# Cross-attention and expert layer: all halves routed four tasks to a slot, six scattered two to a step, and a small buffer cleared behind each scatter of the last two

## What is computed

```python
def reference(x, ctx_768, mask, ...):
    # attention: queries from the normed x; keys and values from the context and from the normed x
    x = x + xattn(ctx_768, layernorm(x), mask, ...)      # 4 heads of 64, key norm, softmax over 77 + 1024 keys
    # experts: each token goes to 8 of 64
    h = layernorm(x).reshape(4096, 256)
    scores = sigmoid(h @ gate_w.T)
    sfc = scores + gate_bias
    group_scores = top_k(sfc by 8 groups of 8, 2).sum()  # the best 4 groups are kept
    topk_idx = top_k(sfc in those groups, 8)
    weights = scores[topk_idx] / sum * 2.5
    pos = running count of the tokens of each expert     # over 256: left out
    buf[e, pos] = h[token]                               # 64 x 256 rows
    y = (silu(buf @ w_gate) * (buf @ w_up)) @ w_down
    return x + add up of y * weight by token
```

## Time and profile before

| what | us |
|---|---|
| median of three runs | 1085.38 (1082.44 to 1087.95) |
| span of the profiled execution | 1168.4 |
| busy in it: TensorE | 906.8 (78%) |
| VectorE | 655.7 (56%) |
| GpSimd | 581.3 (50%), of it the 256 scatters 251.2 |
| ScalarE | 463.0 (40%) |

### The profile page before, as it was taken

The page is one execution under the profiler, slowest core; times in us unless marked ns, Lnnn a source line. Parts: engine busy times, 40 slices in busy tenths (PEclk is TensorE's granted clock), DMA queues, the critical chain, the costliest instruction groups (busy, mean ns, idle before and its releaser), DMA issues.

```text
span 1168.4 us, 13234 instructions
## 1 busy us (share of the span) xinstructions
PE 906.8 (78%) x3848; PEld 626.7 (54%) x3848; DVE 655.7 (56%) x1956; ACT 463.0 (40%) x930; POOL 581.3 (50%) x522
## 2 busy tenths in 40 slices
PE   3869999999999999999964973957308999889300
PEld 2545666556656656656532542846207888777200
DVE  4475647875789775888652743743533443333206
ACT  3734675545755646664430521333103333222000
POOL 3530231204755635655665073155554888888850
PEclk9879999999999999999986995968658999999755
DMA  7739602012221422101261102000428999999689
GB/s 249 267 111 386 218 3 72 20 31 90 77 78 58 132 84 87 55 23 67 78 239 54 37 29 87 24 24 9 171 88 244 308 312 188 158 159 152 70 231 392
DMA packets 85335, 150.77 MB, mean 129 GB/s; under 512 B 14090, under 2 KB 53050, under 8 KB 83216
## 3 DMA queue, kind: packets, MB, share of 16 engines
q1 hardware_dynamic: 54543, 112.32, 27.8%
q0 software_dynamic: 30720, 37.61, 16.3%
HBM read 69.19 MB, written 97.45 MB: 143 GB/s over the span
## 4 chain that ended last, share of the span: by engine, by line
PE 48%; DVE 13%; issue 11%; POOL 8%; another core or an unknown queue 7%; DMA 7%; ACT 4%; POOLq 0%; SPq 0%; ACTq 0%; DVEq 0%
PE ps_o L1257 15%; PE ps_u L1154 6%; POOL sum L1111 4%; PE ps_s L1233 4%; PE ps_s L1235 4%; PE ps_u L1177 4%; DMA out_rows<-again,row_ids 3%; PE ps_u L1269 2%; PE ps_o L1252 2%; POOL out_rows L1111 2%; PE ps_u L1321 2%; DVE mp L1580 2%; PE ps_u L1165 2%; DMA sum<-again,row_ids 2%
## 5 line engine op out<-in xcount | busy, mean ns | idle before, releaser
L1044 POOL DMA_INDIRECT slot_rows<-rows,slot_idx x256 | 251.2, 981 | 312.0 <-issue 137.5
L1580 DVE TENSOR_REDUCE mp<-ps_u 128x1 f32<-128x512 f32 x256 | 165.1, 686 | 103.2 <-remote 49.6
L1450 ACT ACTIVATE probs<-ps_s 128x512 f32<-128x512 f32 x256 | 139.9, 596 | 176.6 <-PE ps_s L1235 105.4
L1111 POOL DMA_INDIRECT sum<-again,row_ids x84 | 130.0, 1548 | 26.5 <-issue 22.6
L1257 PE MATMUL ps_o<-probs,pool 128*128 128x512 f32 (+1 forms) x288 | 138.0, 602 | 2.5 <-ACT den L1471 2.5
L1321 PE MATMUL ps_u<-again 128*128 128x256 f32 x512 | 123.9, 386 | 0.0
L1257 PE MATMUL ps_o<-probs,V 128*128 128x512 f32 (+1 forms) x216 | 106.4, 615 | 10.4 <-ACT probs L1453 5.9
L1235 PE MATMUL ps_s<-qbT,Kb 65*128 65x512 f32 (+1 forms) x252 | 102.4, 406 | 0.0
L1752 DVE TENSOR_SCALAR again<-ps_o,again 128x256 f32<-128x256 f32 x128 | 56.1, 480 | 82.3 <-DMA sum<-again,row_ids 54.7
L1154 PE MATMUL ps_u<-wqkv_s,lnT 128*128 128x512 f32 (+1 forms) x256 | 97.4, 515 | 4.1 <-ACT lnT L1373 3.2
L1321 PEld LDWEIGHTS ps_u<-again 128*128 128x128 f32 x512 | 94.2, 194 | 11.0 <-issue 0.3
(11 more groups left out here) (190 smaller groups left out, 1610.8 us busy)
## 6 DMA issues: line engine op xcount, KB each, us to landing
again<-in_wexp SPq DMA_DIRECT2D x64, 384.0 KB, 5.3
slot_rows<-rows SPq DMA_DIRECT2D x2, 10272.0 KB, 35.0
again<-slot_rows SPq DMA_DIRECT2D x64, 321.0 KB
sum<-rows SPq DMA_DIRECT2D x2, 4352.0 KB, 27.6
again<-sum SPq DMA_DIRECT2D x8, 1024.0 KB, 11.3
Kb<-K SPq DMA_DIRECT2D x16, 275.5 KB
pool<-in_x SPq DMA_DIRECT2D x4, 1024.0 KB, 5.5
xres<-in_x SPq DMA_DIRECT2D x8, 512.0 KB
```

The costliest lines, as they stand in the source:

```text
L1044: pool.indirect_dma_start(out=slot_rows, out_offset=bass.IndirectOffsetOnAxis(ap=slot_idx[x][:, q, k:k + 1], axis=0), in_=rows[x][:, q, :] ...
L1111: pool.indirect_dma_start(out=(out, *sums)[e % PLANES], out_offset=bass.IndirectOffsetOnAxis(ap=row_ids[:, e % RING, t:t + 1], axis=0), in ...
L1450: act.activation(probs[:, n % NPR, hh, :], ps_s[:, u % NSC, :], ACT.Exp).then_inc(s["probs_made"], 1)
L1580: v.tensor_reduce(mp[:, i, tile, half:half + 1], bank((*t, i))[:, :], AX.X, ALU.max).then_inc(s["emptied_vec"], 1)
```

## The change

Three things. `route` puts the tasks of every half four to a slot, and its scatters one to a slot; before, the first five halves went through `chain`, which kept a slot between tasks of different engines. `paced` now holds for six halves, (0, 0) to (2, 1), and begins 9 steps earlier than it did: half n waits from step 18 * (n + 1) + 9 on. And behind each scatter of the halves (3, 0) and (3, 1), but for the last tile of (3, 1), GpSimd clears a buffer `pause` of 128 x 384 numbers that nobody reads, with `link`, so that it waits for the clearing before its next scatter. These are 56 clearings.

```diff
+SCATTER_LAG = 9
...
     def route(self, half, first):
         b, x = half
         tasks = self.route_tasks(b, x)
-        if half < (B - 2, 1):
-            self.chain(tasks, first, [(("scale", b, x, PR - 1, 1), 1)])
-            first = self.at[tasks[-1]] + 1
-        else:
-
-            for n, t in enumerate(tasks):
-                self.slots.setdefault(first + n // 4, []).append(t)
-            first += len(tasks) // 4
-
-        first = max(first, self.last_scatter)
-        pace = 1.0 if half < (B - 2, 1) and x else 0.5
+        for n, t in enumerate(tasks):
+            self.slots.setdefault(first + n // 4, []).append(t)
+            for e, c in COST[t[0]].items():
+                self.load[(e, first + n // 4)] = self.load.get((e, first + n // 4), 0.0) + c
+        first = max(first + len(tasks) // 4, self.last_scatter)
+        pace = 1.0
...
-        if (b, x) < (B - 2, 0):
-            return NKT * PR * (2 * b + x + 2) + (TOPK * q + k) // 2
+        if (b, x) < (B - 1, 0):
+            return NKT * PR * (2 * b + x + 1) + SCATTER_LAG + (TOPK * q + k) // 2
...
+    pause = sb("pause", [P, 384])
...
+                if plan.paced(b, x, q, k) is None and (x, q) != (1, QT - 1):
+                    link(pool.memset(pause[:], 0.0))
```

## The result

The changed kernel takes 1148.0 us (1147.1 to 1148.3, four runs), the kernel before 1085.3 (1082.4 to 1088.0, four runs): the ratio is 1.058, 95% interval 1.0555 to 1.0597. That is slower, as forecast, but by 62.7 us instead of 50.5, and 2 us over the upper end of the range. Its profiled execution has a span of 1146.3 us, 1.8 us less than its own time. The kernel before showed a span 83 us over its timed runs; of such a gap nothing is left.

A forecast was written before the change was run, and what follows sets the result against it. TensorE was taken to pace the first three batches, the scatters to end the last. 1085.4 + 0 (stalls) + 50.5 (clearings) + 0 (denser routing) = 1136 us; the forecast's own range was 1106 to 1146.

The forecast's parts named there:

- f = 0: Share of the scatter bursts' 88 us that timed runs lose too; taken as about 0, so pacing gains them 0.
- 88 us by missing matmuls: Last batch's bursts in the profiled execution: 58 us before the first scatter of (3, 0), 30 in the tail.
- I find no stretch that offers them: Argument on the profiled execution: were the stalls real when timed, some other 83 us would have to be its own.
- real in the timed runs too: Rival on the scatter bursts: timed runs lose the 88 us as well, so the time is 1048 us; chance 0.22.
- The sign of being wrong: For the whole kernel: if the timed run falls with the profiled span, the 83 us were something else.
- The pause: Scatters of (3, 0) and (3, 1): one with its clearing takes 2.20 us instead of 1.28.
- the upper bound of 2.4: Scatter with clearing in the tail: 1.1 us more if the clearing also meets VectorE, a rise of 62 us.
- The tail: From T, the first scatter of (3, 0), to the scatters' end: 140.0 us instead of 89.5, +50.5.
- Denser routing, taken as 0: Batches 0 to 2: same work, counting products 6 or 7 steps earlier; 0 us, with -6 to +10.
- the third rival: Early halves: VectorE's pieces in one run make TensorE wait for `ps_u`; 1146 us, chance 0.04 shared with remaining stalls.

The follow-up runs named there:

- e10: The changed kernel, unedited, in a session with stalls: 1149.3 us against 1162.0 for the kernel before.
- e16: The changed kernel with a clearing behind every fourth scatter only, 14 in all, in a calm session: 1107.0 us, 1.016 of the kernel before.
- e13: The kernel before, unedited, run as the first kernel of its session, which had the stalls: 1160.0 us.
- e18: The changed kernel without its 56 clearings, in a session with stalls: 1139.0 us.
- e5: The kernel before, unedited, as a run of its own in a calm session: 1087.3 us, span 1085.5.
- e4: The changed kernel with the first four halves routed and paced as before, 56 clearings kept: 1189.6 us, 1.018 of the kernel before.
- e1: The kernel before with (2, 0) and (2, 1) paced as in the changed kernel, (2, 0) routed densely, no clearings: 1161.3 us, 0.994.
- e17: The changed kernel with a clearing behind every fourth scatter only, 14 in all, in a session with stalls: 1109.9 us, 0.949 of the kernel before.
- e11: The changed kernel without its 56 clearings, in a session with stalls: 1133.2 us.

## Why the prediction was right or wrong

**Stalls, f = 0: the value right, its ground wrong.** In the timed runs of the result the bursts cost nothing that shows. Not because a timed run is not recorded, but because, by its times, that session was calm. The Trainium skill (NOTIFIC — the notification-queue block, section 7.1), cited for f = 0, explains nothing of it: a recorded execution of the kernel before without a single such wait is at hand (span 1085.5, time 1087.3). The sum of the stalls was well sized: 88 us by missing matmuls, 1168.4 - 1085.5 = 82.9 by the two spans. The step "I find no stretch that offers them" was sound; the step from there to stalls that belong to the profiled execution passed over a third reading, that the two numbers came from sessions of different kinds. For the rival "real in the timed runs too" the number would have been 1149.3 (e10) and not 1048: it subtracted 88 us from a median that had no stalls in it. The sign of being wrong that the prediction named, a timed run that falls with the span, did not come, and yet the 83 us were something else: it could not tell this reading apart.

**One row read wrongly, without consequence.** VectorE's operations of 0.76 us in the earlier trace rows were laid on the burst of scatters. They last as long as GpSimd's residual bias in the earlier trace rows (775.53 to 778.31), and the 0.17 beside them is of half their elements; the same line on 128x32 takes 0.21 at 739.56 in the calm run. That run has such slow ones too, again beside arithmetic of GpSimd:

```profile
489.20 0.76 DVE L1661 TENSOR_TENSOR wsel<-rep 128x64 f32<-128x64 f32 x1
489.14 1.42 POOL L1091 TENSOR_TENSOR QL1b<-pool,st 128x256 fp32r<-128x256 f32 x2
```

They are no part of the stalls.

**The pause: right.** 2.19 us a scatter (2.20 forecast), of it 0.43 clearing (0.41) and 0.78 wait (0.78). No run shows the 1.1 us more that the upper bound of 2.4 gave it: none of the 56 clearings took over 0.44.

**The tail: right.** T + 142.7 (140.0 forecast) against T + 91.9 in the calm run (89.5): +50.8 where +50.5 was said. Both are some 2.5 us longer than worked out, for reasons of their own (and the terms of the 89.5 add up to 89.3): the calm run of before stood 3.76 us behind its residual bias, and in the changed kernel four gaps of 1.1 to 1.9 us between scatters were left, of which I had let the clearings take all.

**Denser routing, taken as 0: this step failed.** With their starts laid on one another (first block's end at 114.21 in the calm run, 116.14 in the changed kernel), T comes 710.18 - 116.14 - (701.35 - 114.21) = 6.9 us later. e16 gives 1107.0 - 1088.0 - 14 x 0.92 = 6.1 by another way, from medians of two calm sessions. The loss arises in the last blocks of batches 1 and 2 (the calm run of before, then the changed kernel):

```profile
394.48:423.59 29.11, 28.25 (x103) 16.54 (x102) 26.16 (x84) 12.40 (x24) 16.14 (x17) 1.00 0.31 104
564.21:593.28 29.07, 27.93 (x100) 15.86 (x98) 26.42 (x85) 11.22 (x20) 16.85 (x18) 1.00 0.20 58
```

```profile
391.43:427.17 35.74, 33.03 (x114) 19.53 (x112) 25.01 (x75) 16.84 (x32) 14.90 (x16) 0.95 0.23 77
566.02:600.79 34.77, 31.81 (x106) 19.42 (x106) 23.49 (x61) 13.68 (x24) 14.76 (x16) 0.90 0.15 43
```

They take 6.6 and 5.7 us longer. The rest of the first three batches gives 6.7 of these 12.3 back, which makes 5.6 by the end of batch 2, and 1.3 more are lost from there to T. Of what is given back, 3.6 lie in a block that the calm run takes 53.6 us for and the trace ahead of the prediction, like e13, 50.0. Against that trace the changed kernel is 8.7 us behind by the end of batch 2, not 5.6. It takes 484.2 to 484.7 us from its first block's end to there in 11 of its 12 traces with and without clearings (487.7 in e18), while the kernel before, with and without clearings, takes 472.6 to 479.1 in six. So the size of this term depends on the run of before that is laid beside it, 6.9 us being that of e5; where the other blocks gain and lose was not followed up.

VectorE in the changed kernel at the turn to the last block of batch 2: the last row maxima are ready at 564.6, but the pieces of the choice (L1669 to L1687) are queued between them and the maximum over them (L1606), whose negation (L1611) goes into the queries' row.

```profile
563.75 0.87 DVE L1600 TENSOR_REDUCE mp<-ps_u 128x4 f32<-128x312 f32 x2
564.54 0.18 DVE L1669 TENSOR_TENSOR gs<-sel 128x32 f32<-128x32 f32 x1
...
566.94 0.61 DVE L1687 MAX8 v<-sfc 128x8 f32<-128x64 f32 x4
567.58 0.18 DVE L1606 TENSOR_REDUCE mx<-mp 128x8 f32<-128x24 f32 x1
567.79 0.17 DVE L1611 TENSOR_SCALAR QL1a<-mx 128x8 fp32r<-128x8 f32 x1
```

TensorE waits for it, then for the carry of the choice; at the turn to the last block of batch 1 it waits for the same row of the other half (third line):

```profile
568.02 1.28 PE L1204 MATMUL ps_u<-ident,QL1a 128*65 128x128 f32 x8 [2.04 <-DVE QL1a L1611]
570.25 0.21 PE L1293 MATMUL ps_u<-selb,tri 128*128 128x64 bf16 x1 [0.95 <-DVE carry L1697]
...
394.53 1.83 PE L1204 MATMUL ps_u<-ident,QL1b 128*65 128x128 f32 x8 [2.71 <-DVE QL1b L1611]
```

Behind the first of these waits, and ahead of the second, its granted clock falls from 1.00 to 0.50, 1.2 GHz, and stays there for some 7 us, one of them idle (stretches of 2 us):

```profile
566.00:568.00 2.00, 0.00 (x0) 0.00 (x0) 1.79 (x12) 1.95 (x4) 0.00 (x0) 1.00 0.00 0
568.00:570.00 2.00, 1.28 (x8) 0.88 (x8) 1.83 (x12) 1.58 (x3) 0.00 (x0) 0.70 0.00 0
570.00:572.00 2.00, 1.75 (x11) 1.56 (x12) 1.90 (x6) 0.05 (x1) 0.00 (x0) 0.50 0.00 0
572.00:574.00 2.00, 2.00 (x6) 1.54 (x5) 1.83 (x9) 1.49 (x3) 0.00 (x0) 0.50 0.72 139
```

Waits of 3 us, and some 6 us of work at half speed, which cost about 3, are the 5.7. In batch 1 it is 2.7 us of waiting and a clock of 0.61 from 395 to 399 us. e4 and e1 bear it out: their first four halves are routed as before and only (2, 0) densely, and up to the last two blocks of batch 2 they keep within 0.5 us of the trace ahead of the prediction. Those two take 75.2 and 75.3 us in them, 75.5 in the changed kernel and 70.6 in that trace, with the clock at 0.50 from 568 to 572 us again. What is not shown by a run is that another order on VectorE would save it. It is the third rival (VectorE's pieces make TensorE wait), only that the wait is for the queries' row and not for `ps_u`; it had 0.04. What spoke for 0 was a row of (2, 1), routed this way already, where TensorE was busy 26.9 of 28 us. But that row was from a stretch between two bursts. It told nothing of how the choice falls in with the last maxima of batches 1 and 2. I had looked at how busy TensorE was, not at what VectorE's order put ahead of the maximum.

**The sum, once more.** From the calm run of before (e5, time 1087.3): +1.9 by the start, +6.9 routing, +50.8 tail, +1.2 experts (293.4 against 292.2) is 1148.1; measured 1148.0. The forecast's 1136.0 lacked the 6.9, the experts' 1.2, and some 4 us by which the start and the baseline of the runs differ. Since the routing's own bounds, -6 to +10, held the 6.9, the 2 us by which the time lies over the range are in part of the range's making: its upper end, 1146, was the forecast with the routing's worst case alone; the bound for the pause (+62 instead of +50.5) was worked out and then not added, and nothing was allowed for what differs between sessions.

**The marks in the profile.** No remote waits from 590 to 700 us: seen in the calm kind, some 11 us of them left in e10. A scatter each 2.2 us: seen. GpSimd without a pause to T + 140: 142.7. TensorE busy over 0.95 to step 107: 0.96 over the stretch, but 0.91 in its last block. The span near the timed run: 1.8 us, and it proves nothing, as in either kind of session span and time of one execution are that close.

## What to carry to other kernels

When the profiled execution and the timed runs disagree by far more than the two us around a span, first ask whether they are of the same session: a second profile of the unchanged kernel, with timed runs of its own session beside it, tells, and a change that is meant against the difference is worth nothing where the difference isn't there. A spacing that is meant to break up bursts needs trying at its sparsest first: here a pause in four scatters did nearly all that one behind each did, for 13 us instead of 51. And before work is packed more densely on VectorE, look at which short, late-needed instruction (here the maximum over the maxima) it puts itself ahead of; TensorE pays the wait twice, the second time in its clock.

Neither of the two kernels that came to both kinds of session, the changed one and the one with 14 clearings, beats the one before in both. The one with 14 clearings is 5% faster with stalls and 1.6% slower without, and varies by 3 us between them, where the kernel before varies by some 75 to 80.

## What the runs showed of the hardware

A burst of indirect scatters from GpSimd, 128 rows each and 1.28 us apart, is harmless in some sessions (159 matmuls in 40 us, 28 scatters in a row) and in others holds ScalarE and VectorE for up to 21 us at a time (37 to 40 matmuls), on the same chip and by the same program. In sessions with stalls the longest single wait was 1.4 to 5.8 us in bursts of 14, 4.8 to 7.6 about those of 19 behind T in the kernel without clearings, 11.5 to 13.8 in those of 16 that followed there, 18.1 in the 22 of e1 and e4, and 13.4 to 21.2 about the two bursts of 28 in the kernel before, with and without clearings. It grows with the length of the burst only roughly, and no length was found from which on it begins. With a pause of 2.19 us behind at most five scatters, one remote wait over 1 us is left in the tails of the eight such traces from sessions with stalls (6.16 us in e17, 2.2 of them unexplained). What it is in the session that decides, and by what way a scatter holds another engine, stays open. That a stall ends with a gap in the scatters looked likely from the earlier trace rows, an exponential at 630.63 us behind a gap at 629.81, but in e11 a wait ended while the scatters went on, 1.28 us apart:

```profile
769.18 0.60 ACT L1447 ACTIVATE probs<-ps_s 128x512 f32<-128x512 f32 x1 [11.48 <-remote]
```

```profile
768.78 0.98 POOL L1041 DMA_INDIRECT slot_rows<-rows,slot_idx  x1 [0.30 <-issue]
770.07 0.97 POOL L1041 DMA_INDIRECT slot_rows<-rows,slot_idx  x1 [0.30 <-issue]
771.34 0.97 POOL L1041 DMA_INDIRECT slot_rows<-rows,slot_idx  x1 [0.30 <-issue]
```
